# Shorter lags between TensorE, ScalarE, VectorE and the store queue in the first SAGE layer of a graph network

## The reference, cut to what matters

```python
def sage(h, w_self, w_neigh, b):
    agg = jax.ops.segment_sum(h[src], dst, num_segments=n) * inv_deg
    return h @ w_self + agg @ w_neigh + b
h = jax.nn.relu(sage(features, ws0, wn0, b0))      # 128 -> 256 features
```

## Time and profile before

| | us |
|---|---|
| median of 3 runs | 5292.63 |
| the three runs | 5287.95 to 5303.60 |
| time of the profiled execution | 5276.13 |
| its span | 5274.4 |
| first and last store issue of `hout` in `sage_first` | 1430.7 and 1966.1 |
| TensorE busy, share of the span | 86% |
| VectorE, ScalarE, GpSimd busy | 69%, 51%, 57% |

### The profile page before, as it was taken

How to read it: one execution, slowest core, us unless ns; L and a number is a source line. 1 busy time by engine, 2 the same in 40 slices (tenths; PEclk the granted TensorE clock), 3 DMA queues, 4 the chain that set the end, 5 groups by cost and what they waited for, 6 DMA issues and landing times. The chain is left out here.

```text
span 5274.4 us, 102984 instructions
## 1 busy us (share of the span) xinstructions
PE 4554.6 (86%) x26356; PEld 3497.7 (66%) x26356; DVE 3618.0 (69%) x11417; ACT 2701.4 (51%) x6655; POOL 3012.1 (57%) x2949
## 2 busy tenths in 40 slices
PE   4499996666699989999999997888789999878777
PEld 4478885555466656676766765777656666777777
DVE  8568776666566645555555564788768888876776
ACT  2645555766444442222222222777777777664555
POOL 0077775777677755444444443777476666007776
PEclk5599998888799999999999998999999999999999
DMA  4889995666599985445455553788877777784554
GB/s 149 288 243 291 285 283 179 197 196 201 190 328 329 329 306 166 171 163 172 165 168 170 165 171 98 231 246 246 241 232 235 236 235 228 260 308 144 152 152 141
DMA packets 576022, 1145.98 MB, mean 217 GB/s; under 512 B 114083, under 2 KB 121034, under 8 KB 572810
## 3 DMA queue, kind: packets, MB, share of 16 engines
q1 hardware_dynamic: 475802, 924.73, 51.4%
q0 software_dynamic: 100080, 219.67, 16.3%
HBM read 705.95 MB, written 438.05 MB: 217 GB/s over the span
## 5 line engine op out<-in xcount | busy, mean ns | idle before, releaser
L881 POOL DMA_INDIRECT s_rows<-t_h,s_index x417 | 519.9, 1247 | 712.4 <-DVE s_index L874 613.4
L881 POOL DMA_INDIRECT g_rows<-t_x,g_index x417 | 418.1, 1003 | 372.0 <-DVE g_index L874 260.2
L881 POOL DMA_INDIRECT cb_rows<-t_x,cb_index x417 | 395.1, 947 | 381.9 <-DVE cb_index L874 257.0
L881 POOL DMA_INDIRECT at_rows<-t_m,at_index x417 | 445.8, 1069 | 260.4 <-DVE at_index L874 151.3
L881 POOL DMA_INDIRECT s_rows<-t_v,s_index x417 | 404.0, 969 | 203.8 <-issue 120.1
L881 POOL DMA_INDIRECT s_rows<-t_x,s_index x417 | 420.6, 1009 | 151.7 <-issue 121.9
L1805 ACT ACTIVATE s_hid<-bank,sb_c 128x512 f32<-128x512 f32 x196 | 124.1, 684 | 731.0 <-PE bank L1778 731.0
L881 POOL DMA_INDIRECT g_rows<-t_h,g_index x417 | 402.6, 965 | 161.1 <-issue 126.5
L947 PE MATMUL bank<-g_onehot,g_rows 128*128 128x168 f32 (+4 forms) x980 | 239.3, 406 | 200.7 <-DMA g_rows<-t_h,g_index 195.0
L1842 DVE TENSOR_TENSOR s_rout<-bank,s_x 128x512 f32<-128x512 f32 x98 | 67.8, 692 | 491.2 <-PE bank L1790 491.2
L947 PE MATMUL bank<-s_onehot,s_hi 128*128 128x168 f32 (+4 forms) x1470 | 350.8, 282 | 56.3 <-DVE s_lo L915 49.3
(11 more groups left out here) (356 smaller groups left out, 12688.1 us busy)
## 6 DMA issues: line engine op xcount, KB each, us to landing
s_scale<-inv_d SPq DMA_DIRECT2D x196, 256.0 KB
htt<-s_ht SPq DMA_DIRECT2D x98, 512.0 KB
t_h<-s_hout SPq DMA_DIRECT2D x98, 512.0 KB
s_ht<-htt SPq DMA_DIRECT2D x98, 512.0 KB
t_m<-s_mout SPq DMA_DIRECT2D x98, 264.0 KB
at_own<-t_m SPq DMA_DIRECT2D x98, 264.0 KB
t_x<-so_x SPq DMA_DIRECT2D x98, 256.0 KB, 4.3
g_own<-t_x SPq DMA_DIRECT2D x98, 256.0 KB
```

The lines of the kernel that those rows point to most:

```text
L881: pool.indirect_dma_start(out=self.rows[:, self.row(q, k), :], out_offset=None, in_=self.table[0:NPAD, :], in_offset=bass.IndirectOffsetOn ...
```

## The change

Five lines of `sage_first` change; every instruction stays, and only the order and the lags move. On TensorE `cross` comes before `dense` and both lags fall by a step or two. On ScalarE `catch` runs at lag 3 in place of 6, `relu` at lag 2 in place of 4, and `take_hi` stands between them instead of last. On VectorE `mean` follows `prepare_split` in the same step, for the same group. SP stores `hout` at lag 6 instead of 7.

```diff
-                    (7, lambda q: store(sp, q, group_of(t_h[0:NPAD, :], q.t), hout[q.u][:, :], caught, stored))])
+                    (6, lambda q: store(sp, q, group_of(t_h[0:NPAD, :], q.t), hout[q.u][:, :], caught, stored))])
...
-                over_groups(pe, [(1, sums), (3, dense), (5, cross)])
+                over_groups(pe, [(1, sums), (3, cross), (2, dense)])
...
-                over_groups(act, [(6, catch), (4, relu), (0, lambda q: e.take_hi(act, q))])
+                over_groups(act, [(3, catch), (0, lambda q: e.take_hi(act, q)), (2, relu)])
...
-                e.on_vector(dve, [(2, mean), (0, lambda q: e.prepare_split(dve, q))])
+                e.on_vector(dve, [(0, lambda q: e.prepare_split(dve, q)), (0, mean)])
```

## The result

The changed kernel takes 5567.9 us in the median (5566.7 to 5571.7, 4 runs) against 5290.3 for the kernel before: a ratio of 1.0528, with a 95% interval of 1.0513 to 1.0542. That is 278 us more. Forecast were 5483 us and a range up to 5560: the side and the loop through the store were right, the size was not, and the time lies 8 us above the range. The profiled execution took 5567.0 us, its span is 5565.3.

A forecast was written before the change was run, and what follows sets the result against it. The prediction took TensorE, DMA and gathers as today's limits and the two-group store loop as the new bound: 195 us over 93 groups, less 5 at the end, on 5292.6 gives 5483 us; range 5425 to 5560.

The forecast's parts named there:

- What bounds the kernel: Phase before the change: TensorE, DMA engines and GpSimd gathers near their limits; closer order saves at most some 0.2 us a group.
- the old store loop: Before the change, `catch` waiting for the `hout` store over three groups asks for 5.58 us a group; bursts stood 5.65 apart.
- Which store `catch` waits for, and the loop over two groups: `catch` waits for the store of two groups earlier; this loop shortens from three groups to two, 7.75 us a group.
- the formula: New pace is 8.39 us plus the time from SP's first issue to `catch`, divided by two groups: 7.75 us.
- L in a drained queue, 7.1: Time from SP's first burst issue to the `catch` waiting for its last DMA: 7.1 us, bounds 4.05 and 8.0.
- the term 8.39: Rest of the new store loop over two groups: hand-overs, `catch`, halves, `sums`, `cross`, `dense` at present speed, 8.39 us.
- a rival with 0.15: TensorE's clock falls to 0.83 through idle time in one or two gaps: +52 us, 5535 us; chance 0.15.
- `relu` hidden: ScalarE's `relu`, 1.27 us, starts with the low halves and is hidden behind low halves and `sums`, 1.97 us.
- VectorE's loop: `sums`, `mean`, one-hots, low halves and hand-overs take 5.5 us a group; the next bound with the store loop gone.
- the rival "the change does nothing": SP's store is not held behind the `xt` load; GpSimd or VectorE sets the pace, 5281 us; chance 0.03.
- VectorE's order costs nothing: `mean` in the same step as the preparation gives a 5.5 us loop, well under 7.75: no cost now.
- The end of the phase: After the last `sums`, TensorE has fewer `dense` and `cross` left: 5.1 us less.

The follow-up runs named there:

- experiment 5: Changed kernel with `cross` and `catch` one step later (lag 4 each) and `hout` stored at lag 5: 5271.2 us, ratio 0.9976.
- experiment 6: Kernel before with only its `hout` store at lag 6 instead of 7: 5280.7 us, ratio 0.9996.
- experiment 7: Kernel before with only ScalarE's order changed, high halves ahead of `relu`: 5281.0 us, ratio 0.9995.
- experiment 1: Changed kernel with SP storing `hout` at lag 5 instead of 6: 5305.3 us, ratio 1.0033.
- experiment 9: Changed kernel with SP storing `hout` at lag 7 instead of 6: 6384.9 us, ratio 1.2076.
- experiment 10: Changed kernel with the `hout` store still at lag 6 but first in SP's step, ahead of the load of `xt`: 5307.0 us, ratio 1.0038.
- Experiment 4: Changed kernel with four `hout` buffers instead of two, store still at lag 6: 5311.0 us, ratio 1.0037.
- Experiment 3: Changed kernel with two extra throwaway matmuls on TensorE ahead of each group's `sums`: 5483.2 us, ratio 1.0363.
- experiment 2: Changed kernel with SP's two stores in the other order, `hout` ahead of `ht`: 5456.4 us, ratio 1.0318.
- Experiment 8: Kernel before with only VectorE's order changed, `mean` behind the preparation of the same group: 5672.7 us, ratio 1.0739.

## Why the prediction was right or wrong

**What bounds the kernel: held.** The phase before was at the limits of TensorE, gathers and DMA; experiments 5, 6 and 7 gain 0.24% at most by removing waits. That the old store loop was itself close to binding did not matter (experiment 6).

**Which store `catch` waits for, and the loop over two groups: held, and shown.** Experiments 1, 9 and 10 move only the store in SP's queue, which makes the loop three groups, one group and three groups long, and the times follow. Experiment 4 lengthens the loop by buffers. Experiment 3 meets the formula to 0.03 us a group.

**L in a drained queue, 7.1: nearly right.** It is 7.34 in the mean of the 43 pairs. At 0.24 us over two groups in 93 steps this is some 11 us.

**The failed step: the term 8.39, with TensorE at full clock inside the loop.** The sum took the loop's TensorE part (1.15 + 0.79 + 3.52) at today's speed and left the clock to a rival with 0.15, which also left open whether the idle time comes "in one or two gaps". In the run the groups pair up: the idle time of two groups comes in one gap, 4.0 us in the mean, and the `sums`, `cross` and the start of `dense` behind it run in large part at half clock, inside the loop. The term measured 10.21 and not 8.39. The bursts are 8.79 us apart and not 7.75, and 93 x 1.04 = 97 us: 1.82/2 x 93 = 85 of them are this term, 11 are L.

Experiment 3 shows the cause by taking it away: with the gap filled the clock is 1.00 and the term is 8.44, though TensorE has 1.7 us more to do in every group, 167 us in all. Between the two kernels lie 0.96 us a group. The slower term is 0.88 of them and L 0.06. So nearly all of the 85 us between them is work at the lower clock; the uneven spacing costs nothing by itself, and has its part only in that it makes one long gap of two. That the clock would have stayed at full speed with two even gaps is not shown: in experiment 2 it fell behind some gaps of 2.5 us and not behind others. Why the pairs arise was not tested either. A loop over two groups ties a group only to the one two before it, so nothing in it evens out the close first groups of the phase; this is argued, not measured.

Of the increase by the profiled executions, 5567 against 5276, 284 us lie up to the last store issue of the phase (1966.1 us before, 2249.9 after), and 7 us behind it, which the change does not explain.

The rival had priced the fall with the clock of 0.83 from another phase, spread over the work: 1.12 us a loop, +52 us (5535). The clock here is 0.89 over the stretch, milder than that, and yet it cost 1.8 us a loop: it was not spread, it fell on just the half of the work that is in the loop. The Trainium skill (TensorE: Matmul & The Clock Gate, Why this matters for your kernels) warns of idle gaps between bursts of matmuls; the trace agrees, with 0.50 after a gap of 4.0 us.

**`relu` hidden: wrong, without effect on the time.** The text let it start with the low halves. It starts at the end of `dense` (1.8 us of waiting a group in experiment 1), and `cross` waits 0.3 to 0.5 us for it. In the changed kernel that lies in the second group of a pair, which has time. It is the next bound once the store loop is gone, and not VectorE's loop, as the forecast had it: 15 to 20 us in experiments 1, 4 and 10. By it the rival "the change does nothing" with 5281 us would have been too low as well.

**VectorE's order costs nothing: right for this change, but for a reason that the text did not give.** Experiment 8 shows that it depends on `dense` having moved too.

**The end of the phase: held.** From the end of the last `sums` to the last store issue of `hout` are 20.5 us before (1945.6 to 1966.1) and 14.3 after (2235.6 to 2249.9): 6.2 us saved where 5.1 were forecast.

## What to carry to other kernels

When lags in a hand-ordered pipeline shrink, write down for each buffer the loop through its release, the queue's own waits included, and count over how many groups it closes: here a loop of some 16.5 us over three groups was hidden, over two it cost 5%, over one 21%. The length of a loop in groups can be bought back by a buffer, a lag, or a place further ahead in the queue, and all three gave the same time. Where a loop leaves the matmul engine idle, price its work inside the loop at the lower clock, and ask whether the gaps will be even or merge into one.

## What the runs showed of the hardware

Adding 1.7 us of TensorE work to each group made the kernel 85 us faster: the granted clock stayed at 1.00 where it was 0.89. A mean clock tells little of the price: at 0.89 over the stretch, all of the slow work stood in the loop that sets the pace. From the first issue of SP's burst of 1.57 MB to the start of the `catch` that waits for it were 7.3 us in the mean with the queue drained (6.9 to 7.9, once 9.3), 7.2 in experiment 3, and 8.0 before the change with the DMA engines at 95%. Moving one 512 KB store behind the one that is waited for took 1.35 us off this mean.
